# One written table of work for all engines in the first cross attention of a two-layer decoder

## The reference, cut to what matters

```python
def _L0_xattn_ref(x, cond, w_q, w_k, w_v, w_out, b_out):
    q = (x @ w_q).reshape(B, SQ, 16, 64)
    k = (cond @ w_k).reshape(B, SKV, 16, 64)
    v = (cond @ w_v).reshape(B, SKV, 16, 64)
    attn = jnp.einsum('bqhd,bkhd->bhqk', q, k) * 64 ** -0.5
    attn = jax.nn.softmax(attn, axis=-1)
    out = jnp.einsum('bhqk,bkhd->bqhd', attn, v).reshape(B, SQ, 1024)
    return out @ w_out + b_out
```

## Time and profile before

| | |
|---|---|
| median of three executions | 3457.3 us (3453.26 to 3458.07) |
| profiled execution, span | 3459.0 us |
| TensorE busy over the span | 91% |
| this stage, steps of the 32 groups | about 808 to 2013 us, 35% of the span |
| in it busy: TensorE, VectorE, ScalarE, POOL | 1192.5, 717.9, 493.9, 911.6 us |
| granted TensorE clock in it | 1.00 |

### The profile page before, as it was taken

The page is one execution under the profiler, slowest core; times in us unless marked ns, Lnnn a source line. Parts: engine busy times, 40 slices in busy tenths (PEclk is TensorE's granted clock), DMA queues, the critical chain, the costliest instruction groups (busy, mean ns, idle before and its releaser), DMA issues. The chain is left out here.

```text
span 3459.0 us, 62575 instructions
## 1 busy us (share of the span) xinstructions
PE 3138.3 (91%) x24201; PEld 1810.0 (52%) x24201; DVE 2354.6 (68%) x4987; ACT 1708.5 (49%) x2102; POOL 1731.8 (50%) x1163
## 2 busy tenths in 40 slices
PE   7999999989999999999999953958989999999797
PEld 3666666644555555555555523846654434444346
DVE  5999999945655665566656556156429978888518
ACT  3888888823434444444444441222234656666641
POOL 5999999814777777777777831322460000000012
PEclk9999999989999999999999976988997999999898
DMA  2000000020000000000000054730021111120101
GB/s 70 6 2 2 2 2 2 26 55 1 4 1 4 1 4 4 1 4 1 4 1 1 1 160 136 239 86 1 1 43 18 18 18 18 18 26 10 33 1 37
DMA packets 65530, 91.51 MB, mean 26 GB/s; under 512 B 9586, under 2 KB 55539, under 8 KB 64371
## 3 DMA queue, kind: packets, MB, share of 16 engines
q1 hardware_dynamic: 61682, 83.17, 9.5%
q0 software_dynamic: 3072, 4.34, 0.7%
q10 hardware_dynamic: 512, 0.26, 0.0%
HBM read 62.34 MB, written 10.65 MB: 21 GB/s over the span
## 5 line engine op out<-in xcount | busy, mean ns | idle before, releaser
L969 DVE TENSOR_REDUCE x0hm<-x0pM 128x1 f32<-128x400 f32 (+1 forms) x1024 | 520.8, 563 | 378.3 <-PE x0pM L871 378.2
L434 POOL TENSOR_SCALAR rows<-rows,mb 128x1024 bf16<-128x1024 bf16 x512 | 567.5, 1119 | 98.1 <-DVE mb L382 98.1
L376 DVE TENSOR_SCALAR_CACHE_REDUCE rows<-pS 128x1024 bf16<-128x1024 f32 x512 | 605.8, 1209 | 2.0 <-PE pS L312 1.5
L445 ACT ACTIVATE prT<-pP 128x1024 bf16<-128x1024 bf16 x512 | 521.9, 1024 | 110.1 <-PE pP L323 92.6
L1433 DVE TENSOR_REDUCE x1hm<-x1pM 128x1 f32<-128x400 f32 (+1 forms) x1024 | 519.1, 567 | 67.4 <-PE x1pM L1319 64.2
L1552 ACT ACTIVATE x1pr<-x1pST 128x1024 f32<-128x1024 f32 (+1 forms) x416 | 403.8, 1022 | 216.1 <-PE x1pST L1371 216.0
L831 POOL TENSOR_TENSOR x0acc<-x0acc,x0pr 128x1024 f32<-128x1024 f32 (+1 forms) x176 | 422.1, 2398 | 110.2 <-ACT x0pr L1080 95.0
L831 POOL TENSOR_TENSOR x0acc<-x0acc,o_nat 128x1024 f32<-128x1024 f32 (+1 forms) x176 | 419.1, 2381 | 72.3 <-ACT o_nat L1080 53.5
L1080 ACT ACTIVATE x0pr<-x0pST 128x1024 f32<-128x1024 f32 (+1 forms) x208 | 212.9, 1024 | 279.6 <-PE x0pST L915 279.6
L1080 ACT ACTIVATE o_nat<-x0pST 128x1024 f32<-128x1024 f32 (+1 forms) x208 | 213.0, 1024 | 278.4 <-PE x0pST L915 278.0
L2666 POOL MEMSET f_tri<- 128x128 f32 x1 | 0.2, 209 | 675.7 <-POOLq L1224 675.7
(11 more groups left out here) (367 smaller groups left out, 5125.2 us busy)
## 6 DMA issues: line engine op xcount, KB each, us to landing
m_w<-in_moe_w1T SPq DMA_DIRECT2D x16, 1024.0 KB
m_w<-in_moe_w2T SPq DMA_DIRECT2D x16, 1024.0 KB, 9.1
acc_d<-m_zero SPq DMA_DIRECT2D x8, 514.0 KB, 9.5
m_acc<-acc_d SPq DMA_DIRECT2D x8, 514.0 KB, 5.6
x1sq<-x1qh SPq DMA_DIRECT2D x32, 128.0 KB, 4.0
x1sk<-x1kh SPq DMA_DIRECT2D x32, 100.1 KB, 3.6
rows_d<-m_xr SPq DMA_DIRECT2D x1, 2176.0 KB, 9.0
g_xN<-in_x SPq DMA_DIRECT2D x1, 2048.0 KB
```

The costliest lines, as they stand in the source:

```text
L376: nc.vector.tensor_scalar(rows[u][:, half * 1024:(half + 1) * 1024], pS[half][:, :], 1.0, None, ALU.mult, ALU.max, accum_out=mx[u][:, half ...
L434: nc.gpsimd.tensor_scalar(r, r, -1.0, mb[u][:, 0:1], ALU.mult, ALU.add).then_inc(s_df, 1)
L445: nc.scalar.activation(prT[u][:, half * 8:(half + 1) * 8, :], pP[half][:, :, :], ACT.Exp, scale=-1.0 / HD ** 0.5).then_inc(s_ex, 1)
L969: emptied(nc.vector.tensor_reduce(hm[g % 2][:, a, t, i % 8 // 2:i % 8 // 2 + 1], bank(name)[:, 0:w], AX.X, ALU.max, negate=True), name)
```

## The change

The rule is replaced by one table, `ORDER`, of 74 words for a group. `order_of(g)` turns it into the list of the group's work, and TensorE, VectorE and ScalarE all walk that list, each taking its own words. POOL and the DMA queue keep their lists. The operations, their counts, shapes, waits and buffers are the same; 32 maxima a group, 16 ahead.

Core of the diff:

```diff
-    def done(g, kt):
-        if g < 0:
-            return MX + AHEAD
-        return min(GROUPS * MX, MX * (g + 1) + AHEAD + ((kt + 1) * MX) // NK)
-    def units_in(g, kt):
-        ...
+    ORDER = (
+        "S0 M M M V-2 V-1 M S1 M M M copy S2 M S3 M M out1 q sum V0 V1 V2 M M S4 stat0 M M S5 stat1 M M "
+        "S6 stat2 M M recip0 V3 V4 recip1 V5 M M recip2 V6 k0 S7 stat3 M M S8 M M S9 M M S10 M M recip3 "
+        "norm V7 V8 M M S11 M V9 V10 k1 out0 M S12").split()
+    def order_of(g):
+        ...
@@ TensorE
-                for n in range(STEPS):
-                    kt = n % NK
-                    scores(n)
-                    for name in units_in(n // NK, kt):
-                        unit(name)
-                    if kt == 1:
-                        values(n - 1)
-                    elif n and kt % 2 == 1 or n and kt == 0:
-                        values(n - 2)
-                        values(n - 1)
+                for g in range(GROUPS):
+                    for name in order_of(g):
+                        if name[0] == "scores":
+                            scores(name[1])
+                        elif name[0] == "values":
+                            values(name[1])
+                        elif name in number:
+                            unit(name)
@@ ScalarE
-                for n in range(STEPS):
-                    exponentials(n)
-                    ...
-                    if n and n % NK == 0:
-                        copy_out(n // NK - 1)
+                        if name[0] == "scores":
+                            exponentials(name[1])
+                        ...
+                        elif name[0] == "copy":
+                            copy_out(name[1])
```

More of the change, by code:

```diff
@@ new lines, in order_of @@
+    def order_of(g):
+        names, i = [], MX * (g + 1) + AHEAD
+        for word in ORDER:
+            kind, at = word.rstrip("-0123456789"), word[len(word.rstrip("-0123456789")):]
+            if kind == "S":
+                names.append(("scores", g * NK + int(at)))
+            elif kind == "V" and g * NK + int(at) >= 0:
+                names.append(("values", g * NK + int(at)))
+            elif kind == "M":
+                if i < GROUPS * MX:
+                    names.append(("max", i))
+                if i % MX == 3 and i > MX and i // MX <= GROUPS:
+                    names.append(("shift", i // MX - 1))
+                i += 1
+            elif kind == "q" and g + 2 < GROUPS:
+                names.append(("q", g + 2))
+            elif kind == "k" and g // 4 + 1 < H // 2 and g % 4 < 2:
+                names.append(("k", g // 4 + 1, 2 * (g % 4) + int(at)))
+            elif kind == "sum" and g >= 1:
+                names.append(("sum", g - 1))
+            elif kind == "out" and at == "0" and g >= 1:
+                names.append(("out", g - 1, 0))
+            elif kind == "out" and at == "1" and g >= 2:
+                names.append(("out", g - 2, 1))
+            elif kind == "recip" and g >= 1:
+                names.append(("recip", g - 1, int(at)))
+            elif kind == "norm" and g >= 1:
+                names.append(("norm", g - 1))
+            elif kind == "copy" and g >= 1:
+                names.append(("copy", g - 1))
+            elif kind == "stat" and g >= GROUPS - 2:
+                names.append(("stat", 4 * (g - GROUPS + 2) + int(at)))
+        return names
@@ L698, in l0_cross_heads @@
     first = [("k", 0, r) for r in range(4)] + [("q", 0), ("q", 1)]
     later = [("v", t, a) for t in range(6, NC_) for a in range(2)]
-    for i in range(done(-1, 0)):
+    for i in range(MX + AHEAD):
         first.append(("max", i))
@@ L707, in l0_cross_heads @@
     last = [("out", GROUPS - 2, 1), ("sum", GROUPS - 1), ("out", GROUPS - 1, 0), ("out", GROUPS - 1, 1)]
-    for name in first + [n for g in range(GROUPS) for kt in range(NK) for n in units_in(g, kt)] + last:
-        number[name] = count
-        count += 1
+    for name in first + [n for g in range(GROUPS) for n in order_of(g)] + last:
+        if name[0] in ("q", "k", "v", "max", "shift", "sum", "out"):
+            number[name] = count
+            count += 1
     with ExitStack() as ctx:
@@ L1028, in _ @@
                     unit(name)
-                for n in range(STEPS):
[L1030 to L1038, removed]
+                for g in range(GROUPS):
+                    for name in order_of(g):
+                        if name[0] == "recip":
+                            reciprocals(name[1], name[2])
+                        elif name[0] == "norm":
+                            normalise(name[1])
+                        elif name[0] == "stat":
+                            statistics(name[1])
+                        else:
+                            unit(name)
                 unit(last[0])
@@ L1091, in _ @@
                                 name)
-                for n in range(STEPS):
-                    exponentials(n)
-                    for name in units_in(n // NK, n % NK):
-                        if name[0] in ("q", "k"):
+                for g in range(GROUPS):
+                    for name in order_of(g):
+                        if name[0] == "scores":
+                            exponentials(name[1])
+                        elif name[0] in ("q", "k"):
                             high(name)
```

## The result

| | before | changed kernel |
|---|---|---|
| median of the executions | 3457.69 us (3453.26 to 3459.84) | 3361.03 us (3357.17 to 3362.82) |
| profiled execution, span | 3459.0 us | 3359.5 us |
| group without k, S12 to S12 | 36.68 us | 33.61 us |
| group with two whole k (seven) | 40.65 us | 37.21 us |
| group whose second k is the short rest of the keys (seven) | 39.33 us | 35.97 us |

The ratio is 0.972, 95% interval 0.9706 to 0.9734. The prediction was 3355 us, in a range of 3335 to 3378 that it stretched up to 3400, from 102 us less on the profiled span; it became 99.5 us less.

The account below looks back on a forecast made before the run. TensorE's list was taken to bound the stage. Savings of 93 us (29 groups at 3.2), 3.5, 2.5 and 3 made 102 off the profiled 3459.0: 3357, median 3355 us; range 3335 to 3378, stretched to 3400.

Parts of the forecast that it names:

- eleven pieces: Stretches of TensorE's list in a group without k, priced from the old timeline: 16.4 us on 64 rows, 17.0 on 128.
- a term apart: 0.15 us a group added for S3 and S9, each expected to wait about 0.1 us for ScalarE.
- Bank waits, about 2.1 us a group: TensorE's waits for VectorE to empty banks of maxima would go, about 2.1 of the 3.2 us gained a group.
- The six places: Where TensorE waited for banks in each old group: three at 0.40 us and three at 0.31.
- where two loads wait: Reason given for a bank wait costing 0.40 us in front of sum or out, against 0.31 elsewhere.
- the 86.7 us in 285 waits: Weight loads' waits for VectorE in the old stage, 0.3 us each, read as bursts of maxima filling banks.
- Fewer runs and odd M, the rest of 3.2: Six runs of V against seven and fewer odd M give what bank waits leave; 0.15 us a run, some 0.2 entering and leaving.
- The sum: Whole-program gain: 93 us from groups 1 to 29, 3.5 from k, 2.5 from group 0, 3 at the end; 102.
- The signs that were named: Right if period 33 to 34 us, weight-load waits for VectorE below 20 us, six V runs, POOL busy 85% to 90%.
- The first (only changes of mode are saved): Rival: maxima still wait elsewhere for banks; only 0.9 to 1.0 us a group saved, 3427 us; chance 0.10.
- The second rival (POOL): Slower: POOL's additions come late for S7 to S10, 2.4 us more a group, 3530 us; chance 0.05.
- the walk through VectorE's queue: VectorE's work followed through one new group: no bank wait over 0.1 us; M31, M39, M41, M43 closest, 0.2 us in hand.

Follow-up runs that it names:

- four-run kernel: Changed kernel with V3 to V6 in one run and V7 to V10 in another behind S7 to S11 in a row: 3382.11 us, ratio 0.9783.

## Why the prediction was right

**The method.** The period was built from start-to-start pieces of the timeline before. All eleven pieces came within 0.15 us, seven of them within 0.03, and the sum was 33.5 against 33.61. Three of the other four are the stretches with a waiting S, for two of which the prediction had its wait in a term apart.

**Bank waits, about 2.1 us a group.** Measured 2.0, by halving the reductions in the kernel before. The six places were right: half reductions give back 0.40 us at each of three (before out, out and sum), 0.29 at two before V, and 0.2 behind the shift, where 0.31 was taken. The price of 0.40 was right but not the reason given for it, "where two loads wait": the row of the second load is as long with half reductions. That also means that the 86.7 us in 285 waits of the argument's beginning held 56.2 us of real waits, and 30 us that do not shrink with VectorE's work. It did no harm, since the sum was made from the pieces and not from the table of waits.

**Fewer runs and odd M, the rest of 3.2.** Measured 1.13, by the two kernels with half reductions. The price in the text, 0.15 for the run and some 0.2 for entering and leaving, agrees with the 0.32 measured for a run that splits a long one. The other 0.8 us (out, q and sum joined, fewer odd M) no run takes apart.

**The sum.** 29 groups gain 3.07 instead of 3.2: 89.0 instead of 93, mostly by the wait of S6. The groups with k gained 3.44 and 3.36, which is 0.37 and 0.29 beyond the others: seven times each is 4.6 instead of 3.5. The first group gained 1.5 instead of 2.5. From the first exponential of group 30 to the last addition it is 66.2 us against 68.7, 2.5 instead of 3. Together 97.6. Some 1.5 us more were gained before the stage's first S, which stands at 808.02 before and at 806.55 after, and not by the change: the k projections ahead of it, which wait for the transfer of their weights in both kernels, start at 751.26 before and at 749.75 after. The total was 102 against 99.5, of which 98 are the change's.

**The signs that were named.** Period 33 to 34 us: yes. V in six runs: yes. Clock 1.00: yes. Waits of weight loads for VectorE below 20 us in all: no, 22.2 in the four rows; but 11.4 of them stay with half reductions, and the 9.2 of out stay under another name. Together with what else VectorE delays they cost 0.05 us a group. POOL busy 85% to 90%: 83%; I had worked that out for the groups without k and forgot that the others are longer.

**The rivals.** The first (only changes of mode are saved) fell: it would have been 3427 us, and the part that it denied is the larger one, 2.0 of 3.1. The Trainium skill, page "TensorEngine Tiling (Array Packing)", section "Key Properties", says that a change of mode drains the engine. The trace agrees in that a change costs time: one run more costs 0.32 us. No row shows the drain itself. The second rival (POOL) fell too: ScalarE waits for POOL once, in the first group.

**What was luck.** That the third reciprocal finds its place behind the shift was seen in the walk through VectorE's queue, but not that this is a reason why six runs beat five. The walk gave four maxima only 0.2 us in hand, which fits that tables with a run less fail on banks and on the product. The 1.5 us from before the stage brought the total nearer to the forecast, by chance.

## What to carry to other kernels

Where one engine's list sets the time, price its pieces from start to start and build the new period from them, then walk the helper engine's queue through it: that gave this period to 0.1 us in 33.5. A wait in the profile that returns with the same length at each change of kind of work (0.3 us here) may not be a wait for the engine it names; halve that engine's work, and see whether the row goes and whether the time falls. Fewer, longer runs are worth something only as long as the helper engine's work still fits between them: with a run less than here each table became slower or no faster.

## What the runs showed of the hardware that was not expected

The normalising product (VectorE, two inputs in SBUF) takes 0.69 us where POOL is idle, at the end of the stage (1925.6), but 1.02 in the median of the changed kernel and up to 2.89 in the kernel with V7 to V10 joined. VectorE and POOL of the four-run kernel:

```profile
1336.09 2.79 DVE L1009 TENSOR_TENSOR x0on<-x0oc,x0rc 128x512 f32<-128x512 f32 x1
```

```profile
1333.47 4.87 POOL L844 TENSOR_TENSOR x0acc<-x0acc,x0pr 128x1024 f32<-128x1024 f32 x2
1338.48 5.17 POOL L844 TENSOR_TENSOR x0acc<-x0acc,o_nat 128x1024 f32<-128x1024 f32 x2
```

The second addition of the first row starts near 1335.95 and ends at 1338.34. The product is issued at 1336.09 and ends at 1338.88, 0.54 us after it; the next pair of additions takes 5.17 us instead of 4.87. In the kernel with V7 to V10 joined it is the same: the product ends at 1334.30, 0.55 us after POOL's row before it. In the changed kernel the product of 1324.73 starts 0.5 us before the end of the addition of 1322.83 (one takes 2.4 us) and is done 0.5 us after it, in 1.00 us. My reading is that the product waits for the addition under way, and the addition behind waits for the product. Then its length depends on where in an addition it is issued, and the 0.98 in the prediction's walk was a lucky phase. It is part of the reason why joined runs late in a group failed.

The Trainium skill, page "SBUF — State Buffer", section "Who interferes with whom", says this: an instruction of VectorE with two SBUF inputs and one of GpSimd that reads SBUF exclude each other for a whole instruction. The rows agree, with the 0.5 us above. No run here took POOL's additions away to show it alone.
